# Sorted edges of a graph layer: four groups of 416 edges and 17 targets in the slot rows, 32 each, instead of two of 896 and 32

## The chip, the cores and the metric

The kernel runs on one core of a Trainium2 chip. The metric is the device time of that core in microseconds, the median of the runs shown. TensorE (PE) multiplies, VectorE (DVE) and ScalarE (ACT) work on tiles, GpSimd (POOL) issues gathers by index, SyncE (SP) issues plain transfers.

## The reference, cut to what matters

```python
def reference(x, src, dst, edge_type_16, L0_gnn_weight):
    # x: 6250 x 64 f32; src, dst: int32; dst is sorted; weight: 16 x 64 x 64
    h = relu(layernorm(x))
    h_src = h[src]
    msg = sum over r of (h_src * (etype == r)) @ weight[r]
    return x + segment_sum(msg, dst, num_segments=6250)
```

There are 200,000 edges, 6,250 nodes and 16 relations. An edge takes the row of its source from h, multiplies it by the 64 x 64 matrix of its relation and adds it to the row of its target.

## The kernel before, in words

**Two ways for an edge.** The first `NS * SEDGE` edges are summed on TensorE ("sorted" edges): a supertile `s` holds `SEDGE` = 7 x 128 = 896 consecutive edges, which have at most 32 different targets in a row (`SW`). The other edges are fetched: 98 blocks of 768, by 583 indirect transfers of 128 rows from a table in DRAM that holds h times every weight matrix (`table`, made at the start), and summed against one-hot targets (`sum_gathered`, L1324).

**A pair of supertiles.** The unit of the main loop is a pair `n` of supertiles, 70 of them. The source nodes are cut into `SQ` = 17 ranges of 384 nodes. For every pair and range there are 128 slot rows; each supertile of the pair owns 64 of them (`CAP`). An edge gets the next free slot of its range and supertile; one that finds no slot is "spilled" and fetched by index (at most 32 for a supertile). So a slot row stands for one edge, in every range.

**The sorting** (two or three pairs ahead) finds the slots: `sort_ranges` (DVE, L805: which range each edge is in, 14 columns of 128 edges x 17), `sort_ranks` (PE, L1158 and L1164: running counts by triangular and all-ones matrices), `sort_slots` (DVE, L818, L820, L812, L825: the rank of each edge and its one-hot slot), `sort_values` (DVE, L858), `sort_permute` (PE, L1173: the source and the key of each slot), `take_z` (ACT, L615: one copy for each supertile's rows), `sort_turn`/`take_rel` (PE, ACT: the sources as a row, written to DRAM and spread to all partitions as `bc` by SP), `rank_spilled`, `permute_spilled` (PE, L1181, L1186, L1197), `sort_spilled` (DVE, L832, L812) and, once for two pairs, `spilled_rows` (DVE, L842 to L848).

**The sums.** For each range, `source_hots` (DVE, L936) makes one-hots of the source of each slot, and `gather` (PE, L1264, 49 matmuls of 128 x 192 for a pair) turns them into rows of h, in three bfloat16 parts of 64 columns. ACT copies them to `msg_s` (`take_messages`, L672). `key_hots` (DVE, L946, 17 for a pair) makes the one-hot of the key of each slot, relation x 32 + target in the window, 16 x 32 = 512 columns (`KEYS`). `sum_sorted` (PE, L1281) multiplies the messages of a slot range with it:

```python
def sums(q, part, half, keys=slice(0, KEYS)):
    for a in range(2):
        rows = slice(a * CAP, (a + 1) * CAP)
        last = pe.matmul(ps[3 + a][half * D:(half + 1) * D, keys], msg_s[rows, u % MB, q % 2, part * D:(part + 1) * D],
                         khot[rows, v % KR, keys], start=q == 0 and part < 2, stop=(q, part) == (SQ - 1, 2))
```

The rows `a` and the output half `half` each take a half of the array, so that four matmuls of 64 x 64 stand side by side in it: part 0 and part 1 of one range are such a set of four, and the third parts of two ranges are another. A pair has 17 + 8.5 = 25.5 sets, 104 matmuls. `take_sums` (ACT, L681) copies the two sum banks to `agg`, after two pairs `weigh` (PE, L1308, L1313) multiplies the four supertiles' sums by the 16 matrices (`GR` = 4 supertiles x 32 targets = 128 columns) into bank 7 or 5, where `sum_gathered` also puts its blocks, and `add_sums` (DVE, L966) adds the bank to `accT`, 32 columns at a place that is read from `base_row` with a register load (L974, L985).

**The order** is written out by hand. On PE, `STREAM` goes through each pair in three pieces `c`: `gather(n, c)`, then a step of sorting, then `sum_sorted` of the piece before, then `sum_gathered`, `sort_permute`, `sort_ranks` or `weigh`. On DVE an iteration `n` makes the slots of pair `n + 2`, then the hots of pair `n + 1`, with `add_sums` between the first `source_hots` and the first five `key_hots`. A table of estimated times in the code (`now += ...`) chooses the matmuls at which POOL is told to issue its next transfer.

Of the kernel before, what the change touches and what calls it, by code (L numbers as in the profile page):

```python
# [8 lines left out]
F16 = mybir.dt.float16  # L9
# [20 lines left out]
def gnn_program(nc, x, src, dst, etype, weight, out):  # L30
# [11 lines left out]
    NS, SJ, SQ, SK, SW, GR = 140, 7, 17, 3, 32, 4  # L42
    CAP = P // 2

    XC = P // GR
    assert XC == SW
# [42 lines left out]
    sum_at = (0, 0, 1, 2)  # L89
# [55 lines left out]
    for i, (n, c) in enumerate(STREAM):  # L145
        if c == 0:
            starts.append(now)
        now += 0.1
# [6 lines left out]
        if i:  # L155
            now += 0.14
            for b in banks_of(*STREAM[i - 1]):
                for q in range(2 * b, min(2 * b + 2, SQ)):
                    now += 0.214
                    spots.append(now)  # L160
                now += 0.214 if 2 * b + 1 < SQ else 0.107
        now += 0.5 * (c == 0 and n > 0) + 0.22 * (permuted(n, c) is not None) + 0.45 * (ranked(n, c) is not None)
# [8 lines left out]
    FIRST, LAST, LANDED, LEAST = 0.0, now - 24.0, 5.0, 1.2  # L171
# [22 lines left out]
    batch = [place[m] // 2 for m in range(NP)]  # L194
    batches = [[m for m in range(NP) if batch[m] == k] for k in range(NPR // 2 + 1)]
    adds_of = lambda k: GR * (k >= 1) + len(batches[k])
    added_by = lambda k: sum(adds_of(i) for i in range(k + 1))

    def target_bank(k):
        return ps[(7, 5)[k % 2]]  # L200

    def sum_place(m):
        at = GR * SW + batches[batch[m]].index(m) * PW
        return slice(at, at + PW)

    assert GR == 4 and GR * SW + max(len(ms) for ms in batches) * PW <= BANK and max(len(ms) for ms in sums_in) <= len(sum_at)


    assert 128 + 2 * SJ * NSB <= 448
    ROW_AT, RANGE_AT, SOURCE_AT, TURN_AT, KEY_LOAD_AT, WINDOW_AT, KEY_AT, KEY_TURN_AT, RELATION_AT = 6, 7, 8, 12, 16, 20, 21, 26, 30  # L210
# [14 lines left out]
    with ctx:  # L225
# [12 lines left out]
        vals = sb("vals", [P, NS, SJ, 4], F16)  # L238
# [6 lines left out]
        spill_z = sb("spill_z", [P, 2, 8])  # L245
        spill_coef = sb("spill_coef", [P, 2, 8])
        spill_terms = sb("spill_terms", [P, 2, 8])
# [3 lines left out]
        win_x = sb("win_x", [P, 2, GR * SW])  # L251
        iota_own = sb("iota_own", [P, GR * SW])
# [10 lines left out]
        min_s, max_s, min_p, max_p = (sb(n, [P, 1]) for n in ("min_s", "max_s", "min_p", "max_p"))  # L263
        base_s, base_p = sb("base_s", [P, 1], I32), sb("base_p", [P, 1], I32)
        base_row = sb("base_row", [1, NS + NP], I32)
        excess = sb("excess", [P, 4])
        min_b, max_b = sb("min_b", [P, 1]), sb("max_b", [P, 1])
        base_b = sb("base_b", [P, 1], I32)
# [30 lines left out]
        U2 = BCR * SQ * P // 2 + MB * ROW + GR * KEYS + PT * CAP // 2  # L299
# [93 lines left out]
        def _(sp):  # L393
# [18 lines left out]
            sp.dma_start(base_row[:, 0:NSA].rearrange("o (s u) -> o s u", u=1), base_s[0:NSA, :]).then_inc(s_row_s, 16)  # L412
# [17 lines left out]
            sp.dma_start(base_row[:, NS:].rearrange("o (s u) -> o s u", u=1), base_p[0:NP, :]).then_inc(s_row_p, 16)  # L430
            for g in range(2, NPR):
# [7 lines left out]
                if g == KEY_LOAD_AT:  # L439
                    sp.wait_ge(s_turn_b, 1)  # L440
                    sp.dma_start(late_b.bitcast(I32), last_supers(etype)).then_inc(s_typ_b, 16)
                    sp.dma_start(late_c.bitcast(I32), last_supers(dst)).then_inc(s_dst_b, 16)
                if g == KEY_TURN_AT:
                    sp.wait_ge(s_base_b, 1)
                    sp.dma_start(base_row[:, NSA:NS].rearrange("o (s u) -> o s u", u=1), base_b[0:NSB, :]).then_inc(s_row_b, 16)
# [16 lines left out]
        def _(pool):  # L462
# [15 lines left out]
            pool.wait_ge(s_const, 8)  # L478
# [80 lines left out]
        def _(act):  # L559
# [18 lines left out]
            def take_turned(n):  # L578

                which, a, b = n // 2, n % 2 * 4, (4, SJ)[n % 2]  # L580
                act.wait_ge(s_turn_s, n + 1)
                seen = ps[6 + n % 2][:, 0:(b - a) * NSA].rearrange("p (j s) -> p s j", s=NSA)
                to = vals[:, 0:NSA, a:b, (0, 1, 3)[which]]
# [24 lines left out]
            def take_z(g):  # L608
# [4 lines left out]
                for a in range(2):  # L613
# [10 lines left out]
            def take_spilled(g):  # L624
# [5 lines left out]
                act.copy(spill_z[:, w % 2, :], ps[6][:, 480:488]).then_inc(s_xzev, 1)  # L630

            def take_last(part):

                act.wait_ge(s_turn_b, part + 1)
                for i, v in (((0, 0), (1, 1)), ((0, 3),))[part]:
                    seen = ps[6][:, 128 + i * SJ * NSB:128 + (i + 1) * SJ * NSB].rearrange("p (j s) -> p s j", s=NSB)
                    act.copy(vals[:, NSA:, :, v], seen).then_inc(s_turned_b, 1)
# [37 lines left out]
            def take_sums(n):  # L675
                act.wait_ge(s_agg, (n + 1) * SQ)
                g = n // 2
                if g >= 1:
                    act.wait_ge(s_fl, g)
                for a in range(2):  # L680
                    act.copy(agg[:, n % 2 * 2 + a, :], ps[3 + a][:, :]).then_inc(s_aev, 1)  # L681

            for n, c in STREAM:
# [5 lines left out]
                if c == 2 and n in (TURN_AT, KEY_TURN_AT):  # L689
                    take_last((TURN_AT, KEY_TURN_AT).index(n))  # L690
# [713 lines left out]
```

## Time and profile before

| | us |
|---|---|
| runs, median (lowest to highest of 3) | 1066.32 (1064.34 to 1066.62) |
| the profiled execution, span from first to last instruction (no other time of it is given) | 1203.7 |
| PE busy in it | 1083.9 (90%) |
| PE weight loads | 740.5 (62%) |
| DVE busy | 938.3 (78%) |
| ACT busy | 450.0 (37%) |
| POOL busy | 682.1 (57%) |
| mean granted TensorE clock | 0.984 of 2.4 GHz |

The profiled execution is 137 us longer than the runs without a profile. Busy shares are unions of the recorded instructions. The chain of waits is given by the profile as 74% PE, 8% "issue" (the engine waited for nothing that the profile shows), 6% DVE, 5% ACT.

### The profile page before, as it was taken

The numbers are of one execution on the slowest core, as the hardware profiler recorded it, in microseconds if no ns is written. First come the engines' busy times: TensorE is split into PE (matmuls) and PEld (weight loads), VectorE is DVE, ScalarE is ACT, GpSimd is POOL, SyncE is SP. The second block draws the span as 40 slices with busy tenths as digits, with TensorE's granted clock in tenths as the row PEclk, the third lists the DMA queues.
The fourth block names the chain that finished last, engine by engine and source line by source line (L and its number), as shares of the span: only waits on it lengthen the run. The fifth ranks groups of instructions, "written<-read, shape, count | busy, mean of one in ns | idle before, by whom it ended". The sixth has DMA issues, their size and how long they took to land.

```text
span 1203.7 us, 39145 instructions
## 1 busy us (share of the span) xinstructions
PE 1083.9 (90%) x15421; PEld 740.5 (62%) x15421; DVE 938.3 (78%) x2773; ACT 450.0 (37%) x1157; POOL 682.1 (57%) x647
## 2 busy tenths in 40 slices
PE   3998999899989889999999999999999999999897
PEld 1445666666666566666666666666666666666665
DVE  7756878897877688788778778878887887888874
ACT  4884333333333333333333333333333333333332
POOL 2213665566666665667666666666665656666630
PEclk9998999999999899999999999999999999999999
DMA  6795222222222122222222122222222222222211
GB/s 173 301 401 186 59 61 59 58 59 59 62 59 59 37 57 59 59 60 58 59 58 57 43 59 58 60 59 58 60 59 60 59 58 59 58 60 59 59 32 56
DMA packets 41739, 93.69 MB, mean 78 GB/s; under 512 B 14572, under 2 KB 14574, under 8 KB 41557
## 3 DMA queue, kind: packets, MB, share of 16 engines
q1 hardware_dynamic: 13850, 42.12, 10.3%
q0 software_dynamic: 19776, 20.29, 9.9%
q10 hardware_dynamic: 7930, 28.76, 6.2%
q8 instruction: 126, 2.06, 0.7%
q14 instruction: 57, 0.46, 0.1%
HBM read 63.52 MB, written 27.59 MB: 76 GB/s over the span
## 4 chain that ended last, share of the span: by engine, by line
PE 74%; issue 8%; DVE 6%; ACT 5%; another core or an unknown queue 3%; DMA 2%; ACTq 1%; POOL 0%; SPq 0%; DVEq 0%; POOLq 0%
PE ps L1281 33%; PE ps L1264 21%; PE ps L1308 6%; PE ps L1324 3%; ACT u L602 3%; PE ps L1173 3%; DVE u L946 2%; PE ps L1164 2%; PE ps L1197 2%; DMA table<-u 1%; DMA w_cat<-weight 1%; PE ps L1158 1%; PE ps L1203 1%; PE ps L1186 1%
## 5 line engine op out<-in xcount | busy, mean ns | idle before, releaser
L529 POOL DMA_INDIRECT u<-table,row_idx x583 | 612.7, 1051 | 411.3 <-PE ps L1264 138.8
L1281 PE MATMUL ps<-u 64*64 64x512 bf16 (+1 forms) x7280 | 466.5, 377 | 18.0 <-issue 16.0
L672 ACT CAST u<-ps 128x384 bf16<-128x384 f32 (+1 forms) x630 | 265.2, 465 | 527.8 <-PE ps L1264 464.2
L946 DVE TENSOR_SCALAR u<-iota_key,z_sb 128x512 bf16<-128x512 f16 x1190 | 359.9, 368 | 70.3 <-PE ps L1281 50.9
L1264 PE MATMUL ps<-parts,u 128*128 128x192 bf16 x3430 | 333.6, 250 | 11.0 <-issue 9.3
L1281 PEld LDWEIGHTS ps<-u 64*64 64x64 bf16 x7280 | 215.0, 106 | 204.7 <-issue 75.9
L1264 PEld LDWEIGHTS ps<-parts,u 128*128 128x128 bf16 x3430 | 280.6, 99 | 41.0 <-issue 38.5
L936 DVE TENSOR_SCALAR u<-u,node_id 128x1152 bf16<-128x1152 f16 (+2 forms) x420 | 184.5, 495 | 0.0
L681 ACT COPY u<-ps 128x512 f32<-128x512 f32 x140 | 75.2, 589 | 109.5 <-remote 76.8
L966 DVE TENSOR_TENSOR accT<-accT,ps 128x32 f32 x238 | 44.8, 188 | 58.4 <-DVE accT L966 23.1
L1308 PE MATMUL ps<-u,w_cat 128*64 128x128 f32 x1120 | 77.4, 277 | 1.7 <-ACT u L681 1.2
L812 DVE TENSOR_TENSOR u<-iota_slot,rank 128x896 f16<-128x896 f16 x70 | 76.4, 1092 | 2.4
L832 DVE SCALAR_TENSOR_TENSOR spill_rank<-ps,spill_mask 128x14 f32<-128x14 f32 x70 | 11.7, 167 | 84.1 <-issue 30.1
L1308 PEld LDWEIGHTS ps<-u,w_cat 128*64 128x64 f32 x1120 | 65.5, 136 | 15.9 <-issue 14.3
L1324 PE MATMUL ps<-u 128*64 128x32 f32 x1166 | 58.2, 226 | 15.4 <-issue 15.2
L1324 PEld LDWEIGHTS ps<-u 128*64 128x64 f32 x1166 | 46.2, 137 | 38.6 <-issue 37.5
L516 POOL DMA_INDIRECT msg_x<-table,spill_row x35 | 48.2, 1377 | 34.4 <-PE ps L1264 19.2
L1115 PE MATMUL ps<-w_cat,hT 64*128 64x512 f32 x196 | 62.7, 670 | 2.7 <-ACT u L602 2.6
L1173 PE MATMUL ps<-spreadv,u 128*128 128x68 f16 x490 | 30.0, 197 | 27.3 <-DVE spreadv L858 13.2
L602 ACT COPY u<-ps 128x512 f32<-128x512 f32 x98 | 50.7, 604 | 7.6 <-PE ps L1115 3.4
L812 DVE TENSOR_TENSOR spill_hot<-iota_slot,spill_rank 128x448 f16<-128x448 f16 x70 | 43.9, 627 | 2.4
L858 DVE TENSOR_TENSOR spreadv<-ranges,vals 128x476 f16<-128x476 f16 x70 | 45.5, 650 | 0.0
(131 smaller groups left out, 656.4 us busy)
## 6 DMA issues: line engine op xcount, KB each, us to landing
u<-rel_dram SPq DMA_DIRECT2D x70, 544.0 KB
table<-u ACTq DMA_DIRECT2D x24, 1024.0 KB, 5.2
u<-table,row_idx POOLq DMA_INDIRECT x583
rel_dram<-rel_row SPq DMA_DIRECT2D x70, 4.2 KB
x_sb<-x SPq DMA_DIRECT2D x2, 448.0 KB
out<-h_sb SPq DMA_DIRECT2D x3, 224.0 KB
out<-h_sb ACTq DMA_DIRECT2D x3, 224.0 KB
msg_x<-table,spill_row POOLq DMA_INDIRECT x35
```

The costliest lines, as they stand in the source:

```text
L529: pool.indirect_dma_start(out=msg_p[:, b, j, :], out_offset=None, in_=table, in_offset=bass.IndirectOffsetOnAxis(ap=row_idx[:, j, m:m + 1] ...
L602: act.copy(t_out[:, i % TRING, t, half * BANK:(half + 1) * BANK], ps[piece_bank(k)][:, :]).then_inc(s_tev, 1)
L672: act.copy(msg_s[:, u % MB, 0:width, :].rearrange("p q c -> p (q c)"), ps[gather_bank(u)][:, 0:width * ROW]).then_inc(s_gev, 1)
L681: act.copy(agg[:, n % 2 * 2 + a, :], ps[3 + a][:, :]).then_inc(s_aev, 1)
L812: return dve.tensor_tensor(there, places, mine, ALU.is_equal)
L936: last = dve.tensor_scalar(hot[:, part % HRING, k, 0:(there - low) * P], bc[:, b, low * P:there * P], node_id[:, k:k + 1], None, ALU.is_equal)
L946: dve.tensor_scalar(khot[:, v % KR, :], iota_key[:, :], z_sb[:, n % 3, 1, q:q + 1], None, ALU.is_equal).then_inc(s_khot, 1)
L1173: last = pe.matmul(ps[6][:, 0:4 * SQ].rearrange("p (a c) -> p a c", a=2), slot_hot[:, j, :], values[:, :, j, :], start=j == 0, stop=j == S ...
L1264: last = pe.matmul(there, hot[:, part % HRING, t - q * SK, at * P:(at + 1) * P], parts[:, t, :], start=t == blocks[0], stop=t == blocks[-1])
L1281: last = pe.matmul(ps[3 + a][half * D:(half + 1) * D, keys], msg_s[rows, u % MB, q % 2, part * D:(part + 1) * D], khot[rows, v % KR, keys] ...
L1308: last = pe.matmul(target_bank(k)[half * D:(half + 1) * D, 0:GR * SW], w_cat[:, r, :], agg[:, :, r * SW:(r + 1) * SW], start=first, stop=r ...
L1324: last = pe.matmul(target_bank(batch[m])[half * D:(half + 1) * D, sum_place(m)], msg_p[rows, m % PRING, j, :], hot_p[rows, m % PHOTS, j, : ...
```

## The change

- A supertile now has 8 x 104 = 832 edges (`SJ` = 8 columns of `TP` = 104 edges), and there are 152 of them in 76 pairs. Each is cut into two groups of 416 edges, with a window of 17 targets for each (`SW` = 17) and a base of its own: a pair has `WINS` = 4 groups. Each group owns 32 slot rows (`CAP`).
- The key has 16 x 17 = 272 columns in place of 512. `sums` goes over four groups of rows, so that eight matmuls of 32 rows x 64 columns stand side by side in the array, in four banks (3, 4, 5, 7). A pair has 208 matmuls in 25.5 sets of eight.
- The banks 5 and 7 are no longer free for targets. `weigh` writes its 8 x 17 = 136 columns behind the keys of the first sum bank and `sum_gathered` behind those of the second; `take_sums` copies these columns with the sums to `agg`, and `add_sums(n - 2)` adds them from there in every pair. A weighed group of two pairs takes eight adds of 17 columns in place of four of 32, with two register loads in place of one.
- `take_sums` makes four copies in place of two and waits for `sum_gathered` and for the adds of two pairs before; `take_z` makes four copies of 32 rows in place of two of 64. The ring of key one-hots has 34 places in place of 22. The blocks of fetched edges are 96 in place of 98, the transfers 575 in place of 583. The times of the table that places POOL's transfers are changed to match.

```diff
-    NS, SJ, SQ, SK, SW, GR = 140, 7, 17, 3, 32, 4
-    CAP = P // 2
+    NS, SJ, TP, SQ, SK, SW, GR = 152, 8, 104, 17, 3, 17, 4
+    WINS = 4
+    CAP, HJ = P // WINS, 2 * SJ // WINS
...
-    KR, HCH, GB, MB = 22, ((0, 9), (9, SQ)), -(-SQ // 2), 9
+    KR, HCH, GB, MB = 34, ((0, 9), (9, SQ)), -(-SQ // 2), 9
-    SEDGE = SJ * P
+    SEDGE = SJ * TP
+    WEDGE = HJ * TP
...
-    sum_at = (0, 0, 1, 2)
+    sum_at = (1, 1, 2, 2)
...
+    AGG = (3, 4, 5, 7)
+    TARGETS = GR * 2 * SW
+    TWIDE = KEYS + TARGETS
+    weighed_in = lambda n: n // 2 - 1 if n >= 2 and n % 2 == 0 else None
...
-                for a in range(2):
+                for a in range(WINS):
                     rows = slice(a * CAP, (a + 1) * CAP)
                     act.copy(z_sb[rows, g % 3, :, :].rearrange("p v q -> p (v q)"),
                              ps[6][rows, a * 2 * SQ:(a + 1) * 2 * SQ]).then_inc(s_zev, 1)
...
-                g = n // 2
-                if g >= 1:
-                    act.wait_ge(s_fl, g)
-                for a in range(2):
-                    act.copy(agg[:, n % 2 * 2 + a, :], ps[3 + a][:, :]).then_inc(s_aev, 1)
+                if n >= 2:
+                    act.wait_ge(s_fl, n // 2)
+                if summed_by(n):
+                    act.wait_ge(s_sump, summed_by(n))
+                if n >= 2 and added_by(n - 2):
+                    act.wait_ge(s_add, added_by(n - 2))
+                for a in range(WINS):
+                    width = KEYS
+                    if a == 0 and weighed_in(n) is not None:
+                        width = TWIDE
+                    if a == 1:
+                        width = KEYS + len(sums_in[n]) * PW
+                    act.copy(agg[:, n % 2 * WINS + a, 0:width], ps[AGG[a]][:, 0:width]).then_inc(s_aev, 1)
...
-                placed(slot_hot, 0, rank[:, :], CAP).then_inc(s_slots, 1)
+                placed(slot_hot, WINS, HJ, 0, rank[0:TP, :], CAP).then_inc(s_slots, 1)
...
+                for half in range(2):
+                    first = half * GR
+                    for i, base in enumerate(bases_of(2 * GR * g + first, GR)):
+                        add(slice(0, P), base, SW, of[:, (first + i) * SW:(first + i + 1) * SW])
+
+            def add_sums(n):
+
+                if weighed_in(n) is not None:
+                    dve.wait_ge(s_aev, WINS * n + 1)
+                    add_weighed(weighed_in(n), agg[:, n % 2 * WINS, KEYS:TWIDE])
+                if sums_in[n]:
+                    dve.wait_ge(s_aev, WINS * n + 2)
...
-                if n % 2 == 0 and n >= 4:
-                    add_sums(n // 2 - 1)
+                if n >= 2:
+                    add_sums(n - 2)
...
                 if n >= 1 and c == 0:
-                    pe.wait_ge(s_aev, 2 * n)
+                    pe.wait_ge(s_aev, WINS * n)
...
-                    for a in range(2):
+                    for a in range(WINS):
                         rows = slice(a * CAP, (a + 1) * CAP)
-                        last = pe.matmul(ps[3 + a][half * D:(half + 1) * D, keys], msg_s[rows, u % MB, q % 2, part * D:(part + 1) * D],
+                        last = pe.matmul(ps[AGG[a]][half * D:(half + 1) * D, keys], msg_s[rows, u % MB, q % 2, part * D:(part + 1) * D],
                                          khot[rows, v % KR, keys], start=q == 0 and part < 2, stop=(q, part) == (SQ - 1, 2))
...
-                    last = pe.matmul(target_bank(k)[half * D:(half + 1) * D, 0:GR * SW], w_cat[:, r, :], agg[:, :, r * SW:(r + 1) * SW],
-                                     start=first, stop=r >= R - 2)
+                    last = pe.matmul(ps[AGG[0]][half * D:(half + 1) * D, KEYS:TWIDE], w_cat[:, r, :], agg[:, :, r * SW:(r + 1) * SW],
+                                     start=first, stop=r >= R - 2 and g == NGR - 1)
```

How the adds stand in DVE's order, in the middle of the program, between the three source one-hots and the first key one-hots of a pair with a weighed group. `TENSOR_LOAD base_row` is the register load of the places, `ISA` the reckoning of an address from a register, `accT<-...` an add. Before:

```order
L936 TENSOR_SCALAR u<-u,node_id 128x1152 x3
L974 TENSOR_LOAD base_row
L966 ISA
L966 TENSOR_TENSOR accT<-accT,ps 128x32
...
L985 TENSOR_LOAD base_row
L966 ISA
L966 TENSOR_TENSOR accT<-accT,ps 128x32
...
L946 TENSOR_SCALAR u<-iota_key,z_sb 128x512 x5
```

Now:

```order
L954 TENSOR_SCALAR u<-u,node_id 128x1152 x3
L984 TENSOR_LOAD base_row
L980 ISA
L980 TENSOR_TENSOR accT<-accT,u 128x17
...
L984 TENSOR_LOAD base_row
L980 ISA
L980 TENSOR_TENSOR accT<-accT,u 128x17
...
L984 TENSOR_LOAD base_row
L980 ISA
L980 TENSOR_TENSOR accT<-accT,u 128x32
L964 TENSOR_SCALAR u<-iota_key,z_sb 128x272 x5
```

Four adds stand behind the first load before and four behind each of the first two loads now; then come the adds of the fetched blocks behind a load of their own, which now stand in every pair, and before in every second one with the blocks of two pairs. The adds themselves read `agg` (one of the tiles called `u`) now, and the bank (`ps`) before.

How the copies stand in ACT's order, in the middle of the program, between the messages of a pair's first and second piece (L672 or L674; the last sums of the pair before are L681 or L691, the slots' values L615 or L618). Before:

```order
L672 CAST u<-ps 128x384 x3
L681 COPY u<-ps 128x512 x2
L615 COPY z_sb<-ps 64x34 x2
L672 CAST u<-ps 128x384 x3
L622 CAST rel_row<-ps 17x128
```

Now:

```order
L674 CAST u<-ps 128x384 x3
L691 COPY u<-ps 128x408
L691 COPY u<-ps 128x304
L691 COPY u<-ps 128x272 x2
L618 COPY z_sb<-ps 32x34 x4
L674 CAST u<-ps 128x384 x3
L625 CAST rel_row<-ps 17x128
```

Eight copies stand where there were four, with 1256 columns of sums and targets in place of 1024 in the pair shown.

## Rows read from the trace of the kernel before

**Rows 1.** The page: its head, and busy time of each engine.

```profile
span 1203.7 us, 39145 instructions
PE 1083.9 (90%) x15421; PEld 740.5 (62%) x15421; DVE 938.3 (78%) x2773; ACT 450.0 (37%) x1157; POOL 682.1 (57%) x647
```

**Rows 2.** Timeline of PE: start us, us, what; first gather of the first and last pair.

```profile
102.62 2.74 PE L1264 MATMUL ps<-parts,u 128*128 128x192 bf16 x16 [0.50 <-ACT key_p L592]
...
1173.92 1.66 PE L1264 MATMUL ps<-parts,u 128*128 128x192 bf16 x18
```

**Rows 3.** The chain in order of time, 618.5 to 633 us: start us, us, what.

```profile
618.70 1.49 PE ps L1264 x18
...
625.99 0.15 PE ps L1186 x6
626.13 0.13 PE ps L1203
626.26 2.07 PE ps L1281 x36
...
629.51 0.31 PE ps L1197 x7
...
631.89 0.21 PE ps L1158
632.09 0.34 PE ps L1164 x6
```

**Rows 4.** Page, groups: line, shapes, count | busy us, mean ns | idle before.

```profile
L946 DVE TENSOR_SCALAR u<-iota_key,z_sb 128x512 bf16<-128x512 f16 x1190 | 359.9, 368 | 70.3 <-PE ps L1281 50.9
...
L1308 PE MATMUL ps<-u,w_cat 128*64 128x128 f32 x1120 | 77.4, 277 | 1.7 <-ACT u L681 1.2
...
L1324 PE MATMUL ps<-u 128*64 128x32 f32 x1166 | 58.2, 226 | 15.4 <-issue 15.2
```

**Rows 5.** Timeline of DVE, 605 to 616 us: the adds.

```profile
607.69 1.14 DVE L966 TENSOR_TENSOR accT<-accT,ps 128x32 f32 x4
609.57 0.83 DVE L966 TENSOR_TENSOR accT<-accT,ps 128x32 f32 x3 [0.73 <-DVE accT L966]
610.32 1.40 DVE L946 TENSOR_SCALAR u<-iota_key,z_sb 128x512 bf16<-128x512 f16 x5
```

**Rows 6.** Timeline of DVE, 616 to 635 us: an iteration without adds.

```profile
619.49 0.39 DVE L818 TENSOR_TENSOR ranks<-ps,ranges 128x238 f32<-128x238 f32 x1
...
620.35 1.09 DVE L812 TENSOR_TENSOR u<-iota_slot,rank 128x896 f16<-128x896 f16 x1
...
622.44 1.37 DVE L936 TENSOR_SCALAR u<-u,node_id 128x1152 bf16<-128x1152 f16 x3
623.73 1.40 DVE L946 TENSOR_SCALAR u<-iota_key,z_sb 128x512 bf16<-128x512 f16 x5
627.31 0.17 DVE L832 SCALAR_TENSOR_TENSOR spill_rank<-ps,spill_mask 128x14 f32<-128x14 f32 x1 [2.18 <-issue]
627.51 0.63 DVE L812 TENSOR_TENSOR spill_hot<-iota_slot,spill_rank 128x448 f16<-128x448 f16 x1
628.05 1.21 DVE L936 TENSOR_SCALAR u<-u,node_id 128x1024 bf16<-128x1024 f16 x3
...
629.44 1.82 DVE L946 TENSOR_SCALAR u<-iota_key,z_sb 128x512 bf16<-128x512 f16 x6
631.42 0.18 DVE L842 TENSOR_TENSOR spill_terms<-spill_z,spill_coef 128x16 f32<-128x16 f32 x1 [0.15 <-ACT spill_z L630]
...
632.59 1.80 DVE L946 TENSOR_SCALAR u<-iota_key,z_sb 128x512 bf16<-128x512 f16 x6 [0.22 <-issue]
```

**Rows 7.** Timeline of ACT around the copies of the sums.

```profile
624.39 1.07 ACT L681 COPY u<-ps 128x512 f32<-128x512 f32 x2 [1.96 <-remote]
...
639.35 0.40 ACT L615 COPY z_sb<-ps 64x34 f32<-64x34 f32 x2
```

**Rows 8.** Timeline of PE, only what runs between 602.512 and 602.527 us.

```profile
602.51 0.41 PE L1281 MATMUL ps<-u 64*64 64x512 bf16 x4
```

More of the change, by code:

```diff
@@ L147, in gnn_program @@
             starts.append(now)
-        now += 0.1
+        now += 0.25
         for q in ranges_of(n, c):
@@ L168, in gnn_program @@
     starts.append(now)
-    FIRST, LAST, LANDED, LEAST = 0.0, now - 24.0, 5.0, 1.2
+    FIRST, LAST, LANDED, LEAST = 0.0, now - 20.0, 5.0, 1.0
     FETCHES = PALL + NGR
@@ L914, in _ @@
                 own = slice(i * XC, (i + 1) * XC)
-                last = dve.tensor_copy(iota_own[own, own], iota_win[own, :])
+                last = dve.tensor_copy(iota_own[own, i * 2 * SW:(i + 1) * 2 * SW], iota_slot[own, 0:2 * SW])
             step(last)
@@ L970, in add_sums, with bases_of, add_weighed @@
+            def bases_of(first, n):
+                _, bases = nc.values_load_multi_w_load_instructions(
+                    base_row[0:1, first:first + n], engines=[dve.engine], min_val=0, max_val=N,
+                    skip_runtime_bounds_check_because="the bases are clamped to it where they are made")
+                return bases
+            def add_weighed(g, of):
+                if g == 0:
                     dve.wait_ge(s_acc0, 8)
                     dve.wait_ge(s_row_s, 16)
-                if (k - 1) * GR == NSA:
+                if g * GR == NSA:
@@ L973, in add_sums @@
                     dve.wait_ge(s_row_b, 16)
-                _, bases = nc.values_load_multi_w_load_instructions(
-                    base_row[0:1, (k - 1) * GR:k * GR], engines=[dve.engine], min_val=0, max_val=N,
-                    skip_runtime_bounds_check_because="the bases are clamped to it where they are made")
-                dve.wait_ge(s_fl, k)
-                if batches[k]:
-                    dve.wait_ge(s_sump, batches[k][-1] + 1)
-                for i, base in enumerate(bases):
-                    add(slice(0, P), base, SW, slice(i * SW, (i + 1) * SW))
@@ L982, in add_sums @@
-                if batches[k]:
-                    if batches[k][0] == 0:
-                        dve.wait_ge(s_row_p, 16)
-                    _, bases = nc.values_load_multi_w_load_instructions(
-                        base_row[0:1, NS + batches[k][0]:NS + batches[k][-1] + 1], engines=[dve.engine], min_val=0, max_val=N,
-                        skip_runtime_bounds_check_because="the bases are clamped to it where they are made")
-                    for m, base in zip(batches[k], bases):
-                        add(slice(0 if len(tiles_of(m)) > 1 else tiles_of(m)[0] % 2 * D, P), base, PW, sum_place(m))
+                for half in range(2):
+                    first = half * GR
+                    for i, base in enumerate(bases_of(2 * GR * g + first, GR)):
+                        add(slice(0, P), base, SW, of[:, (first + i) * SW:(first + i + 1) * SW])
@@ new lines, in add_sums @@
+            def add_sums(n):
[4 more added lines that the diff above has]
+                    dve.wait_ge(s_aev, WINS * n + 2)
+                    if sums_in[n][0] == 0:
+                        dve.wait_ge(s_acc0, 8)
+                        dve.wait_ge(s_row_p, 16)
+                    for m, base in zip(sums_in[n], bases_of(2 * NS + sums_in[n][0], len(sums_in[n]))):
+                        rows = slice(0 if len(tiles_of(m)) > 1 else tiles_of(m)[0] % 2 * D, P)
+                        add(rows, base, PW, agg[rows, n % 2 * WINS + 1, sum_place(m)])
@@ L1323, in sum_gathered @@
                     rows, half = rows_of(m, j), j % 2
-                    last = pe.matmul(target_bank(batch[m])[half * D:(half + 1) * D, sum_place(m)], msg_p[rows, m % PRING, j, :],
-                                     hot_p[rows, m % PHOTS, j, :], start=j < tiles[0] + 2, stop=j >= PJ - 2)
+                    last = pe.matmul(ps[AGG[1]][half * D:(half + 1) * D, sum_place(m)], msg_p[rows, m % PRING, j, :],
+                                     hot_p[rows, m % PHOTS, j, :], start=False, stop=False)
                 last.then_inc(s_sump, 1)
@@ L1347, in _ @@
                     sort_ranks(ranked(n, c))
-                if n >= 2 and n % 2 == 0 and c == weigh_at:
-                    weigh(n // 2 - 1)
+                if c == weigh_at and weighed_in(n) is not None:
+                    weigh(weighed_in(n))
                 if n == NPR - 2 and c == 1:
```

257 lines of the change are left out of this document (127 added, 130 removed).

## Prediction

> **What bounds the kernel now.** I read the page's head and busy times first [rows 1]: PE 90%, DVE 78% of a span of 1203.7 us. That looks like a kernel bound by PE, but the runs without a profile take 1066.3 us, so these shares belong to an execution that is 137 us longer. DVE's 938.3 us of work are 88% of the median. So I asked what each engine needs for one pair with its stalls taken out.
>
> The timeline [rows 2] gives the frame: the first pair's gather begins at 102.6 us, the last pair's at 1173.9, so 69 pairs take 1071.3 us, 15.53 each, with 102.6 us ahead and 29.8 behind. If these 132.4 us hold in a run without a profile too, its pair takes (1066.3 - 132.4) / 69 = 13.54 us.
>
> PE's pair from the chain [rows 3]: 18 gather matmuls take 1.49 us, so 49 take 4.06. A set of four sum matmuls takes 2.07 / 9 = 0.230 us (36 matmuls are nine sets), 25.5 sets 5.87. Sorting takes 0.21 + 0.34 (ranks), 0.31 twice (the two permutes, which have seven matmuls each), 0.15 + 0.13 (spilled ranks, turn): 1.45. The fetched blocks take 58.2 us over 70 pairs, 0.83, and the weighing 77.4 / 70 = 1.11 [rows 4]. The sum is 13.3 us. What makes 15.53 of it in the profile is mostly time in which PE waited for nothing that is shown, such as the 15.2 us before the blocks' matmuls [rows 4]; the median leaves room for 0.2 us of it. So PE is the bound of the real runs.
>
> DVE's pair, by the distances between starts [rows 6]: ranks and their sum 0.86; slots, mask, values and ranges (620.35 to 622.44) 2.09; three source one-hots 1.29; 17 key one-hots at (1.40 - 0.35) / 4 = 0.263, 4.47; spilled slots (627.31 to 628.05) 0.74; three source one-hots and one one-hot of a fetched block (628.05 to 629.44) 1.39, and 0.10 for 0.4 more of the latter; half of 1.17 for the spilled rows, 0.59. The adds [rows 5]: seven take 2.63 us (607.69 to 610.32) with one gap of 0.73 us for the second register load. Spacing is (1.14 - 0.19) / 3 = 0.317, the usual idle part 0.13, so the load costs 0.60. A pair has 3.4 adds, 1.28 us. Last, the key one-hot's mean is 368 ns over 1190 [rows 4] against 350 undisturbed: 17 x 0.018 = 0.31. The sum is 13.1 us. **DVE is 0.2 us behind PE.** A change that takes time from PE alone gets only that.
>
> **The change, part by part, on PE.** The moving part of a set falls from 512 to 272 columns. At the clock's upper level, 2.4 GHz (the mean granted clock is 0.984 of it), 240 columns are 0.100 us, so a set goes from 0.230 to 0.130 and 25.5 sets save 2.55 us for a pair, if eight tiles of a quarter of the rows run as fully side by side as four of a half. For that there is one row: within 15 ns all four matmuls of a set have begun [rows 8]. Ranks go from seven matmuls of 952 columns in all to four of 680, -0.15 us; spilled ranks and permutes +0.05; weighing 136 columns for 128, +0.07; fetched blocks 7.6 tiles for 8.3, -0.07. ACT now makes 4 copies of sums (some 1,200 columns for 1,024) and 4 of slot values: two of each cost 1.07 and 0.40 us [rows 7], so I add 0.25 and 0.28. PE's `rank_spilled` waits for these and has about 0.3 us to spare (copies end about 1.5 us after the sums, PE arrives after a permute and 18 gathers, 1.8): +0.25. PE's pair becomes 13.3 - 2.65 + 0.25 = 10.9 us.
>
> **On DVE.** The two trios of source one-hots (1.37 and 1.21 us, 3456 and 2816 elements) [rows 6] give 0.16 us for 640 elements, 0.25 ns each, so a key one-hot of 272 columns costs 0.263 - 0.060 = 0.203 and 17 save 1.02 us. The slot one-hots cost 1.04 ns an element (1.09 us for 896, 0.63 for 448): 512 for 896 saves 0.40, the spilled ones at 512 for 448 add 0.07. Ranks, their sum and ranges have 272 elements for 238, +0.035 each; values 544 for 476, +0.07. One-hots of blocks -0.03. Together -1.20 us.
>
> The adds go the other way. Two pairs had 4 + 2.8 of them and now have 8 + 2.5. The narrow ones I take at 0.302 us (the 16-element operation at 631.42 takes 0.18, a 32-column add 0.19: nearly all is fixed cost) [rows 5, 6]. By the order of DVE the first load stands behind three source one-hots, which hide it, but the second and third of an even pair stand behind an add, as the one that cost 0.60 did. So (8 x 0.302 + 2.5 x 0.317 + 2 x 0.60) / 2 = 2.21 us a pair, for 1.28: +0.93. Queued behind them are the first five key one-hots, then the spilled slots. DVE's pair is 13.1 - 1.20 + 0.93 = 12.85 us, so its work per pair hardly falls, and there are 76 pairs for 70: 977 us in place of 917.
>
> The other work is covered. POOL has 613 transfers for 618, SP 76 spreads of a row for 70 beside DMA engines mostly idle; POOL's two extra memsets stand ahead of a wait for the weights' load. If POOL's cover went, a late transfer would delay a block's sum by its own length, about 1 us. At the end four more adds and a load (+1.9 us) stand against some 18 cheaper sets (-1.8): 0.
>
> **The sum.** PE 10.9, DVE 12.85: the bound moves to DVE. I take 12.9, with 0.05 for waits, as the two engines no longer compete. The time is 132.4 + 75 x 12.9 = 1099.9, say **1100 us**, 3.2% slower than 1066.3. Against the profiled execution's own 1203.7 us the same sum is (13.54 to 12.9 for 69 pairs, -44; six more, +77) +33 us, if its unexplained stalls stayed as they are; with two times the sum matmuls they may well grow, and I forecast the runs, not the profile. Ends of the unknown terms: a register load hidden wholly (12.25 us a pair, 1051) or as long as its gap with the wait, 0.73 (12.98, 1106); the disturbance of the key one-hots absent (12.55, 1074); waits as large as now, 13.54 - 13.1 = 0.4 (13.25, 1126).
>
> **A rule that speaks against the sets of eight.** The only row with many small matmuls shows six in 0.15 us, 25 ns each [rows 3], though those have 2 to 12 columns and reload 128 x 128 weights each time; the four that begin within 15 ns [rows 8] show less for a burst. If 25 ns held for a long series, eight would take 0.20 us, not 0.113, and a set 0.217. The Trainium skill, "TensorE: Matmul & The Clock Gate", section "Wait — 56ns, not 53.3ns?", says that start to start never drops below about 25 ns; by that a set costs 8 x 25 = 200 ns.
>
> **The rivals.**
> 1. *DVE is bound (forecast)*, 57%: 1070 to 1130.
> 2. *PE's saving arrives*, 24%, faster. For it: the DVE sum is taken from an execution slowed by its profile, and register loads and semaphore steps may be dearer there. If both 0.60 loads hide and the 0.31 of disturbance goes, DVE needs 11.94 us: 132.4 + 75 x 11.94 = 1028; with half of that, 12.4, 1062. I price it at 1045. It decides from a pair of 12.45 us down, (1066.3 - 132.4) / 75. Against it: the distances are steady and 13.1 fits under 13.54 with little to spare.
> 3. *Sets of eight don't run side by side*, 15%, slower still. At 0.217 us a set, PE's pair is 10.9 + 25.5 x 0.087 = 13.1, and with today's 0.2 us of waits 13.3: 1130; if weights of eight tiles follow one another and a set is no faster than now, 0.230 + 0.03, PE needs 14.2: 1197. Then the change does not do what it says. PE also has to be fed 50% more instructions in less time; its unexplained stalls in the profile are a hint that this can fail.
> 4. *No difference*, 4%: loads half hidden, 12.45.
>
> **How the numbers follow.** About 0.2% is what a measurement of this kernel tells from no change (the three runs span 2.3 us). Faster: rival 2, 24%. Same: 4%. Slower: forecast and rival 3, 72%. The range for 8 in 10 takes the forecast's own ends, no difference, the nearer part of rival 2 and the nearer half of rival 3: 1042 to 1150.
>
> **What would show it.** Right: in the profile after, DVE with few waits in the pairs and PE waiting for DVE at `sort_permute` (L1173's successor) or at the key one-hots; key one-hots 0.20 us apart; two gaps of about 0.7 us among the adds of each even pair; PE's 72 sum matmuls in 1.1 to 1.3 us where no stall stands. Wrong: DVE waiting for PE in most pairs (then rival 3, with 72 sum matmuls in 1.9 us or more, or stalls without a cause in the sums); or a time under 1062, which says that DVE's fixed costs are smaller than I read them. If ACT's copies are late, PE's wait at the spilled ranks grows past 0.3 us a pair, and it would show there first.

## The result and the profile after

The changed kernel takes 1105.97 us (median of 4 runs, 1099.61 to 1110.19) against 1066.47 (1064.34 to 1067.0) for the kernel before: a ratio of 1.0373, 95% interval 1.0349 to 1.0398. It is **slower by 3.7%**, 6 us from the forecast and on the forecast's side. The experiments below show that the number came out by luck: two errors of opposite sign nearly cancel, and the longer row of POOL's transfers that sets the time is no term of the sum.

The page of the profiled execution, which took 1110.19 us itself: head and busy times, answering to [rows 1].

```profile
span 1108.4 us, 57958 instructions
PE 958.2 (86%) x24205; PEld 809.6 (73%) x24205; DVE 910.3 (82%) x3137; ACT 530.7 (48%) x1548; POOL 807.5 (73%) x644
```

This execution is not stretched by its profile as the one before was (span 1203.7). An unstretched execution of nearly the kernel before (b_il, below, 1059.9 us) has PE busy for 1006.8, DVE for 933.5 and POOL for 666.6 us, so with the change PE is busy for 49 us less and DVE for 23 less, and POOL for 141 more, with three instructions less. The page's groups, for [rows 4]; columns: busy us, mean ns, idle us before and what ended it.

```profile
L532 POOL DMA_INDIRECT u<-table,row_idx x575 | 740.8, 1288 | 210.7 <-issue 140.5
...
L1305 PE MATMUL ps<-u 32*64 32x272 bf16 (+1 forms) x15808 | 297.2, 279 | 8.4 <-issue 8.2
L964 DVE TENSOR_SCALAR u<-iota_key,z_sb 128x272 bf16<-128x272 f16 x1292 | 280.9, 286 | 8.8 <-DVE win_x L862 6.9
...
L980 DVE TENSOR_TENSOR accT<-accT,u 128x17 f32 (+1 forms) x392 | 71.3, 182 | 65.0 <-DVE accT L980 26.2
...
L1197 PE MATMUL ps<-spreadv,u 104*128 104x136 f16 x304 | 30.9, 224 | 65.5 <-DVE spreadv L872 64.9
L1343 PE MATMUL ps<-u 128*64 128x32 f32 x1150 | 51.9, 230 | 29.9 <-DMA u<-table,row_idx 28.8
```

The first row is the one to see. The same transfer of a tile of 128 rows has a mean of 1044 ns in b_il. The last row is its effect on PE, which waits 28.8 us for landings in all.

The timeline of PE gives the frame, for [rows 2], and the sums.

```profile
102.93 1.30 PE L1288 MATMUL ps<-parts,u 128*128 128x192 bf16 x7 [0.49 <-ACT key_p L595]
...
601.08 1.25 PE L1305 MATMUL ps<-u 32*64 32x272 bf16 x72
602.25 0.54 PE L1343 MATMUL ps<-u 128*64 128x32 f32 x12
...
1078.28 1.66 PE L1288 MATMUL ps<-parts,u 128*128 128x192 bf16 x18
```

75 pairs take 975.4 us, 13.0 each. The 72 sum matmuls are nine sets of eight in 1.17 us, start to start: 0.130 a set, as forecast. The pairs are not alike. Most stand between 10.4 and 14.5 us; the pairs that begin at 354 and 488 us take 22.4 and 21.3, and four take about 18.

The timeline of DVE in an even pair, with its nine adds, for [rows 5].

```profile
599.03 1.37 DVE L954 TENSOR_SCALAR u<-u,node_id 128x1152 bf16<-128x1152 f16 x3
600.32 1.09 DVE L980 TENSOR_TENSOR accT<-accT,u 128x17 f32 x4
601.75 1.15 DVE L980 TENSOR_TENSOR accT<-accT,u 128x17 f32 x4 [0.34 <-DVE accT L980]
603.23 0.19 DVE L980 TENSOR_TENSOR accT<-accT,u 128x32 f32 x1 [0.32 <-DVE accT L980]
603.34 0.49 DVE L964 TENSOR_SCALAR u<-iota_key,z_sb 128x272 bf16<-128x272 f16 x2
```

There are two gaps among the adds, as said, but of 0.34 and 0.32 us, not 0.7. With 0.13 usual between adds, an exposed register load costs 0.20 us and not 0.60.

**POOL is full.** Its 613 transfers (575 and 38 of spilled rows) run from 106.1 to 1079.5 us, 1.59 us each. Their mean is 1.28 us, and at least 0.30 lies between one and the next; so 1.58 of the 1.59 is spent. The timeline of POOL shows the row: each transfer starts 0.30 us after the end of the one before, and 611 of the 612 gaps are within 0.03 us of that.

```profile
605.83 1.12 POOL L532 DMA_INDIRECT u<-table,row_idx  x1 [0.30 <-issue]
607.25 0.94 POOL L532 DMA_INDIRECT u<-table,row_idx  x1 [0.30 <-issue]
608.50 0.95 POOL L532 DMA_INDIRECT u<-table,row_idx  x1 [0.30 <-PE ps L1288]
609.75 0.95 POOL L532 DMA_INDIRECT u<-table,row_idx  x1 [0.30 <-issue]
611.00 2.30 POOL L532 DMA_INDIRECT u<-table,row_idx  x1 [0.30 <-issue]
```

In the profiled execution of before, 618 took 1.73 us each with a mean of 1.07, and a fifth of the stretch was free. That execution is stretched; in b_il they took 1.50 us each with a mean of 1.04, so a tenth was free. The median of one transfer is 947 ns before and after, but 134 of 613 take over 1.8 us, where 16 of 618 did. All 134 overlap a row of three source one-hots, 72 the first row of a pair and 62 the second, and none ends before the last one-hot of its row. Of the 16 of before only one meets such a row. The trace shows one of the long ones: DVE and POOL in the changed kernel.

```profile
573.63 0.72 DVE L872 TENSOR_TENSOR spreadv<-ranges,vals 104x544 f16<-104x544 f16 x1
574.38 0.44 DVE L819 TENSOR_TENSOR ranges<-vals,iota_range 104x272 f16<-104x272 f16 x1
...
574.74 1.37 DVE L954 TENSOR_SCALAR u<-u,node_id 128x1152 bf16<-128x1152 f16 x3
574.76 2.21 POOL L532 DMA_INDIRECT u<-table,row_idx  x1 [0.31 <-issue]
576.03 1.12 DVE L980 TENSOR_TENSOR accT<-accT,u 128x17 f32 x4
577.27 0.95 POOL L532 DMA_INDIRECT u<-table,row_idx  x1 [0.30 <-issue]
```

The transfer that starts beside the three source one-hots ends at 576.97, 0.86 us after the last of the three, nearly the 0.94 that a whole undisturbed one takes. In the kernel before, the like case beside the three of 628.05 [rows 6] is this:

```profile
628.15 1.23 POOL L529 DMA_INDIRECT u<-table,row_idx  x1 [0.97 <-PE ps L1281]
```

It is held up by 0.29 us, less than what was left of the first of its three (0.38 of 0.48 us). The Trainium skill, "SBUF — State Buffer", section "Who interferes with whom", says that GpSimd and VectorE share one pair of ports, held as an exclusive lock for a whole instruction of VectorE in one of its two-port modes, while the other is blocked. By that rule a transfer waits for one instruction: the row of before agrees, the one of after does not, since it waits for three. The two rows are no exceptions: of the transfers that begin within 0.3 us behind the first one-hot of a pair's first row, 28 in the kernel before have a mean of 1.35 us, and 55 in the changed kernel 2.25.

### The profile page after: what moved, and what is told of

The parts are those of the page before. It is cut to its first block, busy times and chain, and to the rows that moved or that the text cites. A ratio compares the mean times of both kernels' runs of the same rounds, so it can differ in the third digit from the quotient of the medians.

```text
span 1108.4 us, 57958 instructions
## 1 busy us (share of the span) xinstructions
PE 958.2 (86%) x24205; PEld 809.6 (73%) x24205; DVE 910.3 (82%) x3137; ACT 530.7 (48%) x1548; POOL 807.5 (73%) x644
## 3 DMA queue, kind: packets, MB, share of 16 engines
q1 hardware_dynamic: 14870, 45.60, 12.3%
## 4 chain that ended last, share of the span: by engine, by line
PE 42%; DVE 26%; issue 12%; ACT 7%; POOL 7%; DMA 5%; DVEq 2%; ACTq 1%; POOLq 0%
PE ps L1288 15%; PE ps L1305 13%; DVE u L964 9%; POOL u L532 6%; DVE u L954 4%; PE ps L1329 4%; ACT u L605 3%; DMA u<-table,row_idx 3%; PE ps L1343 3%; DVE spreadv L872 2%; DVE accT L980 2%; ACT u L691 2%; DMA table<-u 2%; DVE rank L834 2%; PE ps L1210 1%
## 5 line engine op out<-in xcount | busy, mean ns | idle before, releaser
L532 POOL DMA_INDIRECT u<-table,row_idx x575 | 740.8, 1288 | 210.7 <-issue 140.5
L674 ACT CAST u<-ps 128x384 bf16<-128x384 f32 (+1 forms) x684 | 294.5, 465 | 443.5 <-PE ps L1288 433.3
L1305 PE MATMUL ps<-u 32*64 32x272 bf16 (+1 forms) x15808 | 297.2, 279 | 8.4 <-issue 8.2
L964 DVE TENSOR_SCALAR u<-iota_key,z_sb 128x272 bf16<-128x272 f16 x1292 | 280.9, 286 | 8.8 <-DVE win_x L862 6.9
L1305 PEld LDWEIGHTS ps<-u 32*64 32x64 bf16 x15808 | 227.4, 105 | 49.7 <-issue 31.8
L954 DVE TENSOR_SCALAR u<-u,node_id 128x1152 bf16<-128x1152 f16 (+1 forms) x456 | 197.0, 487 | 0.0
L691 ACT COPY u<-ps 128x272 f32<-128x272 f32 (+3 forms) x304 | 102.0, 421 | 60.8 <-PE ps L1305 60.8
L980 DVE TENSOR_TENSOR accT<-accT,u 128x17 f32 (+1 forms) x392 | 71.3, 182 | 65.0 <-DVE accT L980 26.2
L1329 PE MATMUL ps<-u,w_cat 128*64 128x136 f32 x1216 | 90.4, 289 | 6.7 <-issue 5.2
L1343 PE MATMUL ps<-u 128*64 128x32 f32 x1150 | 51.9, 230 | 29.9 <-DMA u<-table,row_idx 28.8
L618 ACT COPY z_sb<-ps 32x34 f32<-32x34 f32 x304 | 54.6, 180 | 22.5 <-PE ps L1197 15.7
L872 DVE TENSOR_TENSOR spreadv<-ranges,vals 104x544 f16<-104x544 f16 x76 | 54.7, 719 | 0.0
```

The costliest lines, as they stand in the source:

```text
L532: pool.indirect_dma_start(out=msg_p[:, b, j, :], out_offset=None, in_=table, in_offset=bass.IndirectOffsetOnAxis(ap=row_idx[:, j, m:m + 1] ...
L674: act.copy(msg_s[:, u % MB, 0:width, :].rearrange("p q c -> p (q c)"), ps[gather_bank(u)][:, 0:width * ROW]).then_inc(s_gev, 1)
L691: act.copy(agg[:, n % 2 * WINS + a, 0:width], ps[AGG[a]][:, 0:width]).then_inc(s_aev, 1)
L872: dve.tensor_tensor(spreadv[0:TP, :, :, :], each, mine.to_broadcast([TP, PT, 2, SQ]), ALU.mult).then_inc(s_vals, 1)
L954: last = dve.tensor_scalar(hot[:, part % HRING, k, 0:(there - low) * P], bc[:, b, low * P:there * P], node_id[:, k:k + 1], None, ALU.is_equal)
L964: dve.tensor_scalar(khot[:, v % KR, :], iota_key[:, :], z_sb[:, n % 3, 1, q:q + 1], None, ALU.is_equal).then_inc(s_khot, 1)
```

## Experiments

All changes are to the changed kernel unless said. The kernel before, run beside them, took 1064.84, 1064.37, 1064.12 and 1066.45 us in the four series.

### 1. Who sets the end

x_fetch fetches no tile 2 of a block:

```diff
+    fetch_of = lambda m: [j for j in tiles_of(m) if j != 2]
-                for j in tiles_of(m):
+                for j in fetch_of(m):
```

> The changed kernel with one of the six tiles of each fetched block not fetched (480 transfers in place of 575; the sums read what stands in the buffer, so the output lacks these edges). Theory D (DVE alone sets the pair): nothing changes, 1100 to 1108 us. Theory P (POOL's stream of transfers, 1.25 us each and about 1.3 more where one meets DVE's source one-hots, is full and sets the end): POOL needs some 820 us in place of 972, DVE with 12.3 us for a pair is next, 132 + 75 x 12.3 = 1055 us.

x_adds leaves out the second four adds of each weighed group and their load, and x_both does both:

```diff
-                for half in range(2):
+                for half in range(1):
```

> The changed kernel with four of the eight adds of each weighed group, and their register load, left out (half of the targets of these edges are not added). Theory D: (4 x 0.305 + 0.2) / 2 = 0.7 us less a pair, 1053 us. Theory P: the transfers are as many as before and the source one-hots meet as many of them, 1095 to 1105 us.

> The changed kernel with both left out: one tile in six not fetched, and four of eight adds. Theory D: as x_adds, 1053 us. Theory P: the two savings only add up once both are gone; DVE then needs 11.6 us a pair, 132 + 75 x 11.6 = 1002 us.

x_sums leaves out the third bf16 part in PE's sums, and b_sums the same in the kernel before:

```diff
-                        sums(q, 0, 0)
                         spot(sums(q, 1, 1))
-                    if len(both) == 2:
-                        for q in both:
-                            sums(q, 2, q % 2).then_inc(s_agg, 1)
...
+                        sums(q, 0, 0).then_inc(s_agg, 1)
```

> The changed kernel with the third bfloat16 part of the messages left out of the sums (8.5 of 25.5 sets a pair, 72 of 208 matmuls). Theories D and P: PE waits for others, nothing changes, 1098 to 1108 us. Theory S (sets of eight and their many instructions hold PE back): 8.5 sets at 0.13 us are 1.1 us a pair, 1020 us.

> The kernel before without the third bf16 part in the edge sums (34 of its 102 sum matmuls a pair left out, about 2 us of TensorE's 13.3 a pair). The prediction's own working (VectorE stands 0.2 us a pair behind TensorE, 13.1): at most 14 us less, 1050 to 1056. L (VectorE's pair was priced too high, since a register load ahead of adds holds it by 0.2 us and not by 0.6): VectorE's pair is 12.3 to 12.6 and the time 1000 to 1035. P (POOL's stream would set the end here as well, at 1.25 to 1.4 us a transfer of 618): 106 + 618 x 1.25 to 1.4, that is 880 to 970, so POOL alone would not stop it.

| kernel | us | ratio to before, 95% interval |
|---|---|---|
| changed | 1105.97 | 1.0373 (1.0349 to 1.0398) |
| x_fetch | 1058.0 | 0.9929 (0.9911 to 0.9947) |
| x_adds | 1114.36 | 1.0457 (1.0433 to 1.0481) |
| x_both | 1042.48 | 0.9799 (0.9778 to 0.982) |
| x_sums | 1098.86 | 1.0328 (1.0278 to 1.0378) |
| b_sums | 1065.96 | 1.0015 (0.9994 to 1.0035) |

96 transfers less give 48 us; half of the adds less give nothing, the time even rises, by 8 us and to 9 above P's range. POOL's row rises with it: its transfers have a mean of 1.30 us there and the row takes 985 us in place of 973. So DVE's adds are off the path and POOL's row of transfers is on it. PE is not: its busy time falls by 65 us in x_sums, though its granted clock is lower (0.932 in the profiled execution, for 0.966), the time differs from the changed kernel's by less than the intervals tell, and PE waits longer for DVE instead. The busy line and the wait at `sort_permute` in x_sums:

```profile
PE 893.6 (82%) x18733; PEld 748.0 (68%) x18733; DVE 909.5 (83%) x3137; ACT 539.8 (49%) x1548; POOL 795.9 (73%) x644
...
L1197 PE MATMUL ps<-spreadv,u 104*128 104x136 f16 x304 | 32.5, 232 | 132.0 <-DVE spreadv L872 132.0
```

x_both fell between its two expectations, 16 us below x_fetch, where P expected 53. Its transfers still have a mean of 1.28 us, so the hold-ups had not gone with the load; what bounds it is open.

b_sums misses both the prediction's own working and L. From its page:

```profile
PE 920.3 (87%) x12901; PEld 663.7 (62%) x12901; DVE 940.5 (88%) x2773; ACT 466.3 (44%) x1157; POOL 684.9 (64%) x647
...
L1173 PE MATMUL ps<-spreadv,u 128*128 128x68 f16 x490 | 28.1, 199 | 109.2 <-DVE spreadv L858 108.9
```

PE is busy for 86 us less than in b_il (920.3 for 1006.8), 1.2 us a pair and not the 2 expected, at a lower granted clock (0.948 for 0.993). Nothing came of it: PE waits for DVE at `sort_permute` for 108.9 us, where b_il has 17.3. So PE's work alone did not set the time of the kernel before. DVE's chain there, waits included, takes (1065.96 - 132.4) / 69 = 13.5 us a pair, not 13.1. PE had next to nothing to spare either: between the first gathers of b_il's first and last pair it is busy for 911 of 929 us. The two chains were equally long.

### 2. Taking the three source one-hots apart

y_il2 puts two key one-hots after the first and two after the second source one-hot; b_il does that to the kernel before:

```diff
                                              node_id[:, k:k + 1], None, ALU.is_equal)
+                    if between is not None and k < SK - 1:
+                        key_hots(n, between + k * 2, between + (k + 1) * 2)
```

> The changed kernel, whole, with VectorE's three source one-hots of each half no longer one behind the other: two key one-hots stand after the first and two after the second, taken from the groups that followed; no instruction is added or left out. F (the row of three holds a transfer of POOL up by 1.1 to 1.5 us, and POOL's full row of transfers sets the end): the transfers' mean falls from 1288 ns towards 1.0 to 1.1 us, and the time from 1106 to 1055 to 1070, where the kernel with a sixth of the block's transfers left out stood (1058). D (VectorE's own work sets the end, as forecast): 1100 to 1110. H (each of the source one-hots holds POOL by itself, whatever stands between): the transfers' mean stays by 1.29 us and the time within 10 us of 1106.

> The kernel before with the same two key one-hots between its source one-hots. All of F, D and H say no difference here, 1060 to 1070, because POOL is not the bound before (411 us idle between transfers) and no work is added; more than 10 us either way would say that the order itself moves TensorE's waits, and y_il2 would then have to be read against it.

y_il2 took 1214.09 us, 1.1363 (1.131 to 1.1417): all three theories are wrong, and by 100 us. b_il took 1062.27, 0.9978 (0.9961 to 0.9995), as expected. The groups of POOL, first of y_il2, then of b_il:

```profile
L532 POOL DMA_INDIRECT u<-table,row_idx x575 | 844.9, 1469 | 208.6 <-issue 142.4
```

```profile
L529 POOL DMA_INDIRECT u<-table,row_idx x583 | 608.6, 1044 | 288.9 <-issue 117.8
```

With 0.30 between, 613 transfers of a mean of 1.455 us are 1076 us, and the stretch from the first to the last is 1079. POOL's row fills the stretch to 3 us. The same edit leaves the transfers of before as they were. The timeline of y_il2 shows why they grow:

```profile
604.09 0.72 DVE L872 TENSOR_TENSOR spreadv<-ranges,vals 104x544 f16<-104x544 f16 x1
604.58 2.92 POOL L532 DMA_INDIRECT u<-table,row_idx  x1 [0.30 <-issue]
604.85 0.44 DVE L819 TENSOR_TENSOR ranges<-vals,iota_range 104x272 f16<-104x272 f16 x1
...
605.21 0.51 DVE L954 TENSOR_SCALAR u<-u,node_id 128x1152 bf16<-128x1152 f16 x1
605.63 0.48 DVE L966 TENSOR_SCALAR u<-iota_key,z_sb 128x272 bf16<-128x272 f16 x2
606.03 0.51 DVE L954 TENSOR_SCALAR u<-u,node_id 128x1152 bf16<-128x1152 f16 x1
606.46 0.48 DVE L966 TENSOR_SCALAR u<-iota_key,z_sb 128x272 bf16<-128x272 f16 x2
606.86 0.51 DVE L954 TENSOR_SCALAR u<-u,node_id 128x1152 bf16<-128x1152 f16 x1
```

The transfer ends at 607.50, 0.13 us after the last source one-hot (607.37). A longer row of one-hots holds it up longer, and the key one-hots between, which hold nothing by themselves (88 transfers of the changed kernel meet only those, with a mean of 0.95 us), do not let it go. So in the changed kernel something holds POOL over a whole row of source one-hots, and in the kernel before nothing does (of b_il's 292 transfers that meet source one-hots none takes over 1.5 us), though these are the same instructions with the same widths.

### 3. What differs: addresses, or partitions

Two things differ around these instructions. The buffers lie 32 bytes off, taken modulo 64; and a group of 416 edges on each of four makes the sorting's operations work on 104 partitions, where they had all 128. y_pad moves the buffers:

```diff
+        pad = sb("pad", [P, 8])
         u1 = sb("u1", [P, HOTC + KHOTC])
```

> The changed kernel, whole, with 32 bytes a partition left free ahead of the buffer of one-hots, so that the source one-hots, the rows that they read and what lies behind stand at the same remainder of 64 bytes as in the kernel before. A (where the source one-hots lie decides whether a row of three holds a transfer up for its whole length): the transfers' mean falls from 1288 ns to 1.05 to 1.10 us as in the kernel before, and the time to 1050 to 1070. Q (it is the operations on 104 partitions) and every theory that does not turn on addresses: no difference, 1100 to 1110.

y_128 lets `sort_ranges`, `placed` (slots and spill places) and `sort_values` run on 128; the added rows of `vals`, `rank` and `spill_rank` are set to 0 once:

```diff
-                qids = vals[0:TP, 2 * g:2 * g + 2, :, 0:1].rearrange("p s j v -> p (s j) v").to_broadcast([TP, PT, SQ])
-                dve.tensor_tensor(ranges[0:TP, :, :], qids, repeat(iota_range[0:TP, :], PT), ALU.is_equal)
+                qids = vals[:, 2 * g:2 * g + 2, :, 0:1].rearrange("p s j v -> p (s j) v").to_broadcast([P, PT, SQ])
+                dve.tensor_tensor(ranges[:, :, :], qids, repeat(iota_range[:, :], PT), ALU.is_equal)
```

> The changed kernel with VectorE's two-input operations of the sorting (ranges, slots, spill places, spread values) on all 128 partitions as in the kernel before, where the change has 104 (the added 24 rows are of no use to anyone); the same instructions with the same widths. Q (an operation with two SBUF inputs on a part of the partitions lets the following row of source one-hots keep POOL out for its whole length): the transfers' mean falls to 1.05 to 1.10 us and the time to 1050 to 1070. A (addresses): no difference, 1100 to 1110.

y_pad took 1105.04 us, 1.0392 (1.0358 to 1.0425): addresses are out. y_128 took **1061.53 us, 0.9976 (0.9958 to 0.9995)**: 44 us less than the changed kernel, with more work in it. Its page:

```profile
span 1057.9 us, 57962 instructions
...
PE 934.8 (88%) x24205; PEld 796.3 (75%) x24205; DVE 912.8 (86%) x3139; ACT 531.4 (50%) x1548; POOL 663.2 (63%) x645
...
L534 POOL DMA_INDIRECT u<-table,row_idx x575 | 595.4, 1035 | 297.3 <-issue 125.1
...
L1203 PE MATMUL ps<-spreadv,u 104*128 104x136 f16 x304 | 30.7, 223 | 75.0 <-DVE spreadv L878 74.6
```

DVE's busy time is what it was (912.8 and 910.3), POOL's falls by 144 us. No transfer takes over 1.8 us. The timeline at the place within a pair that was shown above, in an earlier pair:

```profile
332.64 0.72 DVE L878 TENSOR_TENSOR spreadv<-ranges,vals 128x544 f16<-128x544 f16 x1
333.39 0.44 DVE L825 TENSOR_TENSOR ranges<-vals,iota_range 128x272 f16<-128x272 f16 x1
...
333.75 1.37 DVE L960 TENSOR_SCALAR u<-u,node_id 128x1152 bf16<-128x1152 f16 x3
333.77 1.05 POOL L534 DMA_INDIRECT u<-table,row_idx  x1 [0.31 <-issue]
```

The transfer begins 0.02 us after the one-hots, as there, and takes 1.05 us in place of 2.21; 23 transfers that begin so have a mean of 1.05 us, for the 2.25 of 55. DVE's rows differ in one thing: 128 for 104. The last transfer ends at 1029.5 us and not 1079.5. Transfers of 1.035 us with 0.30 between fill 818 us of 919, and PE waits for DVE again. Which of the four operations is to blame was not tried, nor whether 96 or 64 partitions do the same. The hold-ups stand at both rows of a pair, the one behind the values and ranges and the one behind the spill places. The operations that read PSUM or one input alone (`ranks`, its sum, the mask) stayed on 104 partitions in y_128, so they are not what makes the hold-ups.

### 4. What the change is worth without it

With POOL free the pairs may be fewer and the blocks more. w_148 and w_144 are y_128 with the base registers of the eight adds loaded ahead of the source one-hots, and

```diff
-    NS, SJ, TP, SQ, SK, SW, GR = 152, 8, 104, 17, 3, 17, 4
+    NS, SJ, TP, SQ, SK, SW, GR = 144, 8, 104, 17, 3, 17, 4
-    FIRST, LAST, LANDED, LEAST = 0.0, now - 20.0, 5.0, 1.0
+    FIRST, LAST, LANDED, LEAST = 0.0, now - 20.0, 5.0, 0.8
```

(148 and 1.0 in w_148).

> The kernel y_128, whole, with 148 groups of edges in place of 152 (74 pairs of 76; 3328 edges and 26 transfers move to the fetched blocks), and with the base registers of the eight adds loaded ahead of the source one-hots. VectorE's work sets the end there at about 12.4 us a pair, and POOL has 297 us of idle time: two pairs less are 25 us, the loads 0.3 us on every second pair (11 us), and the four more fetched blocks cost VectorE and TensorE 4 x 1 to 4 x 3 us: 1030 to 1045. If POOL were the bound, 638 transfers of 1.6 us would give 1150.

> The same with 144 groups of edges, 72 pairs and again some 26 transfers more, and the least space between two signs for transfers in the order of work 0.8 in place of 1.0. Below w_148 by up to 20 us if VectorE still sets the end, 1010 to 1035; above it, 1040 to 1070, if 664 transfers at their least spacing of 1.25 to 1.4 us (830 to 930 us of the stretch of 900) have become the end.

z_148 had 148 groups too, but on top of y_il2, before the cause was known:

> The changed kernel, whole, with the source one-hots apart as in y_il2, the base loads of the eight adds issued ahead of the source one-hots, and 148 groups of edges in place of 152, which makes 74 pairs of 76 and moves 3328 edges to the fetched blocks (26 transfers more). F: POOL has the room, and two pairs less with 0.2 us less on every second pair give 1020 to 1045. D: two pairs of 12.9 us less from 1106, 1075 to 1085. H (POOL is as full as before and has 25 transfers more of 1.59 us): 1120 to 1150.

z_148 took 1164.58 us, 1.093 (1.089 to 1.0969), with transfers of a mean of 1330 ns: POOL's fullness again, above even H's range. w_148 took 1053.87 (0.9896, 0.9862 to 0.993), 9 us over its range and spread by 10 us over its runs. The loads ahead are one reason why it gained only 8 us. DVE's waits in it:

```profile
DVE accT L986 <- DVE accT L986: 16.2, 44, 0.5
DVE u L960 <- issue: 14.1, 33, 0.7
```

The waits between adds are 16.2 us, for 27.1 in y_128, and 14.1 us of waits ahead of the source one-hots are new: the loads' time only moved. The rest of the gap is open. w_144 took **1037.04 us, 0.973 (0.9702 to 0.9759)**, between its two expectations (to 1035 if DVE sets the end, from 1040 if POOL does), and beats both kernels. POOL's row is full again there: 658 of its 662 gaps are within 0.03 us of the least, and 663 transfers from 110.0 to 1005.3 us take 1.35 us each. By that row, more blocks for fewer pairs would gain little more there; it was not tried. Four pairs of 12.3 us less would be 49 us, and 24 of them arrive.

## Why the prediction was right, and where it was not

- **The frame** held: 102.9 us ahead and 1108.4 - 1078.3 = 30.1 behind, for 102.6 and 29.8.
- **"So PE is the bound of the real runs"** fell. b_sums takes 1.2 us a pair off PE's busy time and gains nothing; DVE's chain was as long as PE's, 13.5 us, and not 0.2 shorter.
- **PE's sets of eight** were right, at 0.130 us a set. Rival 3 and its rule of 25 ns are out: 72 matmuls in 1.17 us are 16 ns each, and where a rule and this row differ, the row decides. PE's pair was nearly right too: for 10.9 us, PE is busy for 838 us in the 75 pairs of y_128, 11.2 each.
- **DVE's one-hots** were right: key one-hots stand 0.20 us apart.
- **The adds** were mis-sized: 2 x 0.20 us for the loads of an even pair, not 2 x 0.60, so 0.4 us a pair less. The 0.60 was read from the kernel before and holds there (35 gaps of 0.68 us in b_il, 0.55 above the usual); why a load costs less in the changed kernel is open. The smaller load alone makes 12.45 of the 12.85, the point at which the text put no difference; y_128's timeline gives 12.3 (75 pairs from 106.2 to 1028.3 us). Against the real 13.5 of before, DVE won 1.2 us a pair, enough to pay for six more pairs.
- **The step that failed is "The other work is covered. POOL has 613 transfers for 618"**, with the cover's loss priced at "its own length, about 1 us" for a late transfer. The count was right and the cover gone: a transfer costs 0.24 us more than in y_128 (1.28 for 1.04), which fills POOL's row and adds 44 us to what the change gives otherwise. "The bound moves to DVE" is thus not what happened: it moved to POOL. That the forecast lies within 6 us is luck: its pair was priced 0.6 us too dear on DVE (12.9 for 12.3, 45 us over 75 pairs), and POOL's hold-ups added 44. With the four kinds of operations on all 128 partitions the time is 1061.5 us, and the forecast would have been 38 us off, on the other side.
- Of what was to show the forecast right, PE's wait for DVE at `sort_permute` did (65 us, under 1 a pair), and misled: that wait was there, and longer, in x_fetch and y_128 as well, which were faster.

## What to carry to other kernels

When an instruction's shape changes, look at what other engines do beside it: VectorE's operations cut from 128 to 104 partitions took no less time here (the slot one-hots 694 ns both ways) and made POOL's transfers a quarter longer (1035 to 1288 ns). Where POOL issues transfers, try such operations on all 128 partitions, even with rows of no use. And call an engine's work covered only after dividing its stretch by its operations, the gap between two included.

## What the runs showed of the hardware

- With VectorE's two-input operations on 104 partitions ahead of a row of source one-hots, a POOL transfer that meets the row is kept out until its last one-hot (2.21 us for 1.05 with the same operations on 128; 134 such transfers for none). The port lock that the Trainium skill describes in "SBUF — State Buffer", section "Who interferes with whom", fits the place, but says nothing of partitions; why their number matters is open.
- The transfers cost 1.25 us from start to start when nothing holds them (0.94 and 0.30), so an engine that the page of the changed kernel shows busy for 73% was full.
- A register load exposed between adds cost 0.20 us in the changed kernel and 0.55 in the kernel before (b_il).
